# Q of two batches as fp32r products with late-loaded shared weights, and a transposed integer tail

## The chip, the core and the metric

The kernel runs on one core of one Trainium2 chip. The metric is the device time in microseconds (us) of one execution; lower is better. Five engines work side by side and wait for one another through semaphores: TensorE (PE; its weight loads are listed as PEld), VectorE (DVE), ScalarE (ACT), GpSimd (POOL) and SyncE (SP), which only issues transfers. Each engine runs its own instructions in their order.

## The reference, cut to what matters

Sixteen batches of 112 tokens of width 256 (`x`), each with a context of 375 rows (`ctx_1024`), pass four stages:

```
x = x + attention(layernorm(x), ctx, Wq, Wk, Wv, Wo) + bo     # 16 heads of 64
x = x + expert_ffn(layernorm(x)) + shared_ffn(layernorm(x))   # hidden 1024
x = x + softmax(layernorm(x) @ ctx.T / 16, masked) @ ctx      # one head of 256
x = x + int8_linear(layernorm(x))
```

The last line finds one scale for the whole tensor (the largest magnitude of the normalised x, over 127), divides and rounds to integers, multiplies by an int8 weight, and multiplies each output column by `x_scale * weight_scale` before the bias is added.

## The kernel before

**Attention.** One batch has two halves, c = 0 and 1, of eight heads each; half number u = 2b + c. While a half computes scores, softmax and the mix with V, TensorE also projects Q, K and V for the next half. These projections are cut in eight units of one PSUM bank each: unit 0 is Q (`Q_UNIT`, L1624 to L1631), units 1 to 4 are K, 5 to 7 are V (L1633 to L1649). Even units use bank 0, odd units bank 1. K and V are done as three fp32r products of high and low parts (`split_products`), so their weights and the context are kept as a high and a low part each. Q is one plain fp32 product: four pairs of heads times two row tiles, with the tokens `xn_t` of one batch (112 columns) moving. A Q or K unit is evicted by ScalarE (high part, L754 and L756) and then VectorE (low part, L1099 and L1103); both halves of the bank's release go through `proj_used`.

A half has two visits v = 0 and 1 of four heads each. In each, TensorE does the scores (L1662), the mix of the visit before (L1696), and then four times: transposes of one head's probabilities (`turn_probs`, L1677) and one unit. After visit 1 come the output projection (L1717), which waits for `heads_split`, that is for VectorE's `heads_rest` (L1129), and a turning of tokens (L1609). Head i's transposes wait for the copy of an earlier head out of the bank (L1671 to L1675): head 1 for VectorE's first copy (L1123).

VectorE's list in a visit is fixed by `batch` at L1147: maxima of two heads (L1112), in visit 0 of c = 1 the statistics of layernorm 2 and the context's low part (`ctx_rest`, L1018), maxima of the other two, copies of turned probabilities, reciprocals, the units' low parts, small steps of layernorm 2 (`norm2_steps`), `heads_rest`, and at the end the update of x (L1135). GpSimd multiplies the probabilities by the reciprocals (L664), two heads' worth after each pair of reciprocals, and in visit 1 of c = 1, from batch 2 on, it also issues the scatter of tokens (L672) between the first and the second of its four products.

The batches are unrolled for b = 0, 1 and 15; b = 2 to 14 is a loop of one batch.

**FFN.** The shared weights (`FFN_PIECE`, `FFN_PIECE + 1`) are loaded into `stage` and split in batch 0: `piece_hi` on ScalarE (L741) and `piece_lo` on VectorE (L1010), two halves for each piece. The tokens of the first FFN segment are split by `split_shared(0)` at L1218, in the last batch's c = 0.

**Tail.** The second attention runs one batch t a step; VectorE then does the statistics and extremes of layernorm 4 (`last_stats`). After it: moments, thirteen small steps (`norm_op`), a GpSimd all-reduce, scales, quotients (L980 on ScalarE, L1556 on VectorE), clipping and rounding (`quantise`, L1564 and L1569), transposes (L1993), integer products with tokens as the stationary side (L2006), the scale on VectorE (L1577) and the sum with `x_biased` on GpSimd (L726) or VectorE (L1586). `x_biased` is x plus bias, made on GpSimd (L705). Each of the four groups of four batches goes through this chain.

## Time and profile before

| | us |
|---|---|
| median of three runs | 957.97 (956.17 to 958.02) |
| profiled execution, its own time | 958.77 |
| its span, first to last instruction | 956.0 |
| TensorE busy | 903.7 (95%) |
| VectorE busy | 623.0 (65%) |
| ScalarE busy | 525.6 (55%) |
| GpSimd busy | 268.2 (28%) |

The profiled execution took 2.77 us more than its span, and 0.80 us more than the median. A profile lists, for each instruction, its start and length, and for idle time of an engine what ended it. The first attention fills the span from about 24 to 667 us, the FFN up to about 868, the second attention up to about 925, the tail the rest.

### The profile page before, as it was taken

What the parts mean: (1) busy time and instruction counts of PE and PEld (TensorE: products, weight loads), DVE (VectorE), ACT (ScalarE), POOL (GpSimd) and SP (SyncE); (2) the same over time, 40 slices, a digit from 0 to 9 for tenths busy, and PEclk for the clock granted to TensorE, in tenths of its full rate; (3) what the DMA queues carried; (4) which work ended last, traced back from release to release, by engine and by line L of the source; (5) the groups of instructions that cost most, each with busy time, mean ns of one, the idle gap of its engine ahead of it and who ended that gap; (6) DMA issues with size and microseconds to landing.
All of it is one profiled execution on the core that took longest, in us unless ns stands there. A gap on an engine that the chain in (4) does not pass through costs nothing.

```text
span 956.0 us, 19821 instructions
## 1 busy us (share of the span) xinstructions
PE 903.7 (95%) x6730; PEld 794.5 (83%) x6730; DVE 623.0 (65%) x1634; ACT 525.6 (55%) x1258; POOL 268.2 (28%) x337
## 2 busy tenths in 40 slices
PE   5889999999999999999999999998989999998864
PEld 4779888898888988889898898887878999996643
DVE  6766666767667676676766767665654666348777
ACT  4655565555655556555565555654742555446633
POOL 1323333333333333333433334333100000041214
PEclk9999999999999999999999999999999999999985
DMA  9230000000000000000000000000550142265502
GB/s 290 97 106 17 2 18 5 21 16 5 16 5 21 16 5 16 5 21 16 5 16 5 21 14 7 0 5 9 162 190 20 54 169 85 63 193 163 155 6 77
DMA packets 29459, 50.56 MB, mean 53 GB/s; under 512 B 2480, under 2 KB 24080, under 8 KB 27648
## 3 DMA queue, kind: packets, MB, share of 16 engines
q1 hardware_dynamic: 27888, 46.42, 15.6%
q0 software_dynamic: 1536, 3.67, 1.3%
q8 instruction: 21, 0.34, 0.2%
q14 instruction: 14, 0.11, 0.0%
HBM read 41.83 MB, written 8.26 MB: 52 GB/s over the span
## 4 chain that ended last, share of the span: by engine, by line
PE 88%; DVE 7%; ACT 2%; issue 2%; DMA 1%; POOL 0%; DVEq 0%
PE bank L1648 27%; PE bank L1677 10%; PE bank L1841 9%; PE bank L1696 9%; PE bank L1861 8%; PE bank L1662 8%; PE bank L1630 6%; PE bank L1717 5%; PE bank L1950 2%; PE bank L1968 1%; DVE norm_stats L1023 1%; PE bank L1811 1%; PE bank L1609 1%; PE bank L1957 1%; DMA x_all<-in_x 1%
## 5 line engine op out<-in xcount | busy, mean ns | idle before, releaser
L664 POOL TENSOR_TENSOR probs<-probs,row_rcp 112x375 f32<-112x375 f32 x256 | 202.4, 813 | 415.8 <-DVE row_rcp L1118 415.3
L784 ACT ACTIVATE probs<-bank,neg_max 112x375 f32<-112x375 f32 x256 | 144.4, 570 | 69.0 <-DVE neg_max L1112 68.9
L1677 PE MATMUL bank<-ident,probs 112*125 112x112 f32 x768 | 129.1, 277 | 2.3 <-DVE probs_t L1123 2.3
L1677 PEld LDWEIGHTS bank<-ident,probs 112*125 112x125 f32 x768 | 113.8, 187 | 18.2 <-issue 3.3
L1112 DVE TENSOR_REDUCE neg_max<-bank 112x1 f32<-112x375 f32 x256 | 123.3, 539 | 7.6 <-PE bank L1662 7.5
L1123 DVE COPY probs_t<-bank 125x336 f32<-125x336 f32 x128 | 64.7, 506 | 70.1 <-PE bank L1677 66.8
L756 ACT ACTIVATE k_parts<-bank 128x376 fp32r<-128x376 f32 x128 | 62.1, 485 | 69.3 <-PE bank L1648 69.3
L1648 PE MATMUL bank<-ctx_hi,wk_hi 128*128 128x376 f32 x256 | 97.2, 380 | 2.3 <-DVE k_parts L1103 1.5
L759 ACT ACTIVATE v<-bank 125x512 f32<-125x512 f32 x96 | 57.4, 598 | 57.2 <-PE bank L1648 57.1
L1696 PE MATMUL bank<-probs_t,v 125*64 125x112 f32 x1536 | 87.7, 263 | 0.6 <-ACT probs_t L772 0.6
L1696 PEld LDWEIGHTS bank<-probs_t,v 125*64 125x64 f32 x1536 | 74.0, 137 | 16.9 <-issue 16.7
L1103 DVE TENSOR_TENSOR k_parts<-bank,k_parts 128x376 fp32r<-128x376 f32 x128 | 69.9, 547 | 27.8 <-ACT k_parts L756 27.5
L1648 PE MATMUL bank<-ctx_lo,wk_hi 128*128 128x376 f32 x256 | 85.5, 334 | 0.0
L1648 PE MATMUL bank<-ctx_hi,wk_lo 128*128 128x376 f32 x256 | 85.3, 333 | 0.0
L1648 PE MATMUL bank<-wv_hi,ctx_hi 128*125 128x512 f32 x192 | 83.5, 435 | 0.0
L1662 PE MATMUL bank<-k_parts,q_parts 64*112 64x376 f32 x768 | 82.1, 345 | 0.0
L1648 PE MATMUL bank<-wv_hi,ctx_lo 128*125 128x512 f32 x192 | 75.8, 395 | 0.0
L1648 PE MATMUL bank<-wv_lo,ctx_hi 128*125 128x512 f32 x192 | 75.6, 394 | 0.0
L1662 PEld LDWEIGHTS bank<-k_parts,q_parts 64*112 64x112 f32 x768 | 61.2, 171 | 12.6 <-issue 7.9
L1412 DVE TENSOR_TENSOR hid_lo<-hid,hid_hi 128x448 fp32r<-128x448 f32 x72 | 45.0, 625 | 39.4 <-ACT hid_hi L915 34.2
L1630 PE MATMUL bank<-xn_t,wq_sb 128*128 (+1 forms) x512 | 65.9, 284 | 3.1 <-DVE x_all L1135 2.6
L1630 PEld LDWEIGHTS bank<-xn_t,wq_sb 128*128 128x128 f32 x512 | 62.9, 200 | 3.9 <-DVE x_all L1135 2.8
(208 smaller groups left out, 1877.0 us busy)
## 6 DMA issues: line engine op xcount, KB each, us to landing
stage<-in_ffn_up SPq DMA_DIRECT2D x6, 1024.0 KB, 5.4
stage<-in_ffn_down SPq DMA_DIRECT2D x6, 1024.0 KB, 7.5
ctx_raw<-in_ctx_t SPq DMA_DIRECT2D x16, 375.0 KB, 3.4
ring_late<-in_ctx_t SPq DMA_DIRECT2D x10, 375.0 KB, 6.8
ring_late<-in_ctx_n SPq DMA_DIRECT2D x10, 375.0 KB
routed<-xn SPq DMA_DIRECT2D x1, 2240.0 KB, 11.1
rows_in<-routed SPq DMA_DIRECT2D x5, 448.0 KB, 6.1
answers<-y_rows SPq DMA_DIRECT2D x10, 224.0 KB, 2.7
```

The costliest lines, as they stand in the source:

```text
L664: eng.tensor_tensor(probs[s][:, :], probs[s][:, :], row_rcp[:, s:s + 1].broadcast_to([S, C]), ALU.mult).then_inc(probs_ready, 1)
L784: eng.activation(probs[r][:, :], SCORE_BANKS[i][0:S, 0:C], ACT.Exp, bias=neg_max[:, r:r + 1], accum_out=row_sum[:, r:r + 1]).then_inc(exp_ ...
L1103: eng.tensor_tensor(k_parts[cf][:, 1, k - K_UNIT, :], bank[k % 2][:, 0:CP], k_parts[cf][:, 0, k - K_UNIT, :].bitcast(F32), ALU.subtract) \
L1112: eng.tensor_reduce(neg_max[:, r:r + 1], SCORE_BANKS[k][0:S, 0:C], AX.X, ALU.max, negate=True) \
L1123: eng.tensor_copy(probs_t[i][:, :, :], turn_bank(i, project)[0:CJ, 0:JT * S] .rearrange("p (j s) -> p j s", j=JT)).then_inc(probs_t_ready[ ...
L1630: m = eng.matmul(bank[0][:, p * S:(p + 1) * S], wq_sb[:, kt, col:col + P], xn_t[:, kt, bf, :], start=(kt == 0), stop=(kt == KT - 1))
L1648: m = eng.matmul(dest, wp, ap, start=(n == 0), stop=(n == 3 * KT - 1))
L1662: m = eng.matmul(SCORE_BANKS[2 * p + e][0:S, 0:CP], q_parts[c][heads[e], a, 2 * v + p, :], k_parts[c][heads[e], b, 2 * v + p, :], start=(i ...
L1677: t = eng.transpose(turn_bank(i, project)[0:CJ, j * S:(j + 1) * S], probs[QUAD * v + i][:, j * CJ:(j + 1) * CJ], ident[0:S, 0:S])
L1696: m = eng.matmul(HEADS_BANK[DH * e:DH * e + DH, (s // 2) * S:(s // 2 + 1) * S], v_sb[c][:, j, s * DH:(s + 1) * DH], probs_t[2 * p + e][:, ...
L1841: mm = eng.matmul(bank[n % 3][:, 0:GT], wp, ap, start=(i == 0), stop=(i == 3 * KT - 1))
L1861: mm = eng.matmul(down_banks(s)[k][:, 0:GT], wp, ap, start=(m == 0 and i == 0), stop=(m == MT - 1 and i == 2))
```

## The change

1. **Q of two batches.** From batch 2 on, Q is made for batches b and b + 1 together, as three fp32r products with 224 columns moving, in two units (`PAIR_UNIT` = -1 and `Q_UNIT` = 0) of two pairs of heads each. A pair of batches has four halves; the projections done in them are then of 9, 7, 7 and 9 units (in the order even c = 0, even c = 1, odd c = 0, odd c = 1), where before each had 8. In a half of 7, K stands in the first slot, and the last slot has none; in a half of 9 the last slot holds V units 6 and 7. Tokens are normalised and turned two batches ahead; ScalarE writes their high part (`pair_out`), VectorE their low part (`pair_rest`), which is put right after the first two maxima of visit 0 in c = 1. The loop body is two batches.
2. **Shared weights late.** The split Q and K weights live where the FFN's shared weights go. The split of Wq takes the place of the first piece's in batch 0; the second piece's in batch 0 goes away. The first piece is split at the end of batch 14, the second in visit 0 of the last half, where `split_shared(0)` now also stands.
3. **Tail.** The moments of layernorm 4 are taken inside the loop over t. The integer weights become the stationary side, four products of 448 columns for each group in place of eight of 256. ScalarE scales and adds the bias in one instruction, TensorE turns the result back by fp32 transposes, VectorE adds it to x. GpSimd keeps only the product of the two scales.

```diff
@@ units and order
+                    self.queries = 2 if r % 4 < 2 else 0
+                return {1: [[k] for k in range(8)],
+                        2: [[PAIR_UNIT], [Q_UNIT], [1], [2], [3], [4], [5], [6, 7]],
+                        0: [[1], [2], [3], [4], [5], [6], [7], []]}[self.queries]
@@ scalar, batch
-                        if first and v == 1:
-                            piece_hi(FFN_PIECE + c)
+                        if first and c == 0 and v == 1:
+                            for h in range(2):
+                                eng.activation(piece_half(wq_hi, h), piece_half(wq_sb, h), ACT.Copy) \
+                                   .then_inc(wq_rounded, 1)
...
+                        elif v == 1 and t is not None:
+                            pair_out(t, t % 2 if isinstance(t, int) else odd)
...
+                        if isinstance(b, int) and b == B - 2 and c == 1 and v == 1:
+                            piece_hi(FFN_PIECE)
+                        if last and c == 1 and v == 0:
+                            piece_hi(FFN_PIECE + 1)
@@ vector, batch
                         largest_scores(visit, v, 0)
+                        rest = rest_for(b, c)
+                        if v == 0 and rest is not None:
+                            pair_rest(rest, rest % 2 if isinstance(rest, int) else odd)
...
-                        if first and v == 1:
-                            piece_lo(FFN_PIECE + c)
+                        step_rest(3)
+                        if isinstance(b, int) and b == B - 2 and c == 1 and v == 1:
+                            piece_lo(FFN_PIECE)
...
-                        if last and c == 0 and v == 1:
-                            eng.wait_ge(proj_ready[0], unit_count(u + 1, 4))
+                        if last and c == 1 and v == 0:
+                            eng.wait_ge(proj_ready[1], units.all(1))
                             split_shared(0)
+                            piece_lo(FFN_PIECE + 1)
@@ tensor, unit
+                if k <= Q_UNIT and f.queries == 2:
+                    for i in range(2):
+                        col = (PAIRS * cf + 2 * (k - PAIR_UNIT) + i) * P
+                        for kt in range(KT):
+                            w = [t[:, kt, col:col + P] for t in (wq_hi, wq_lo)]
+                            a = [t[:, kt, :] for t in (xq_hi, xq_lo)]
+                            for wp, ap in split_products((w, a)):
+                                m = eng.matmul(bank[k % 2][:, 2 * i * S:2 * (i + 1) * S], wp, ap, start=(n == 0),
+                                               stop=(n == 3 * KT - 1))
@@ tail
-        VECTOR_RATIOS = (2, 2, 1, 1)
+        VECTOR_RATIOS = (2, 2, 2, GB)
...
+            def answers_out(i):
+                for part in (slice(0, GT),) if i < NG - 1 else (slice(0, 2 * S), slice(2 * S, GT)):
+                    for k in range(KT):
+                        eng.activation(out_t[i][:, k, part], bank[2 * (i % 2) + k][:, part], ACT.Identity,
+                                       scale=out_scale[:, k:k + 1], bias=qb_col[:, k:k + 1]).then_inc(out_t_ready, 1)
...
+            def add_answers(i):
+                for h in range(2):
+                    b = GB * i + 2 * h
+                    eng.wait_ge(out_turned, 2 * i + h + 1)
+                    eng.tensor_tensor(result[i][:, 2 * D * h:2 * D * h + 2 * D].rearrange("s (b d) -> s b d", b=2),
+                                      x_all[:, b:b + 2, :], bank[4 + h][0:S, :].rearrange("s (b d) -> s b d", b=2),
+                                      ALU.add).then_inc(result_ready, 1)
...
+                for n in range(KT):
+                    for k in range(KT):
+                        m = eng.matmul(bank[2 * (i % 2) + n][:, 0:GT], wi[:, k, n * P:(n + 1) * P],
+                                       xi_t[i % 2][:, k, :], start=(k == 0), stop=(k == KT - 1))
+            for i in range(NG):
+                turn_integers(i)
+                if i >= 1:
+                    products(i - 1)
+                if i >= 2:
+                    turn_answers(i - 2)
+            products(NG - 1)
+            turn_answers(NG - 2)
+            turn_answers(NG - 1)
```

## Rows read from the trace of the kernel before

**Rows 1.** The page: busy time and share of each engine, and the last chain.

```profile
PE 903.7 (95%) x6730; PEld 794.5 (83%) x6730; DVE 623.0 (65%) x1634; ACT 525.6 (55%) x1258; POOL 268.2 (28%) x337
...
PE 88%; DVE 7%; ACT 2%; issue 2%; DMA 1%; POOL 0%; DVEq 0%
```

**Rows 2.** Timeline, TensorE, one half c = 1: start us, length us, engine, line, operation.

```profile
407.97 1.27 PE L1662 MATMUL bank<-k_parts,q_parts 64*112 64x376 f32 x12
...
410.89 1.95 PE L1630 MATMUL bank<-xn_t,wq_sb 128*128 x16
412.67 0.49 PE L1677 MATMUL bank<-ident,probs 112*125 112x112 f32 x3
...
416.87 1.30 PE L1662 MATMUL bank<-k_parts,q_parts 64*112 64x376 f32 x12
```

**Rows 3.** The same timeline, neighbouring fp32r products, one after the other.

```profile
406.97 0.28 PE L1717 MATMUL bank<-wo_hi,heads_hi 128*112 128x256 f32 x1
407.09 0.28 PE L1717 MATMUL bank<-wo_lo,heads_hi 128*112 128x256 f32 x1
...
413.53 0.33 PE L1648 MATMUL bank<-ctx_hi,wk_hi 128*128 128x376 f32 x1
413.70 0.34 PE L1648 MATMUL bank<-ctx_lo,wk_hi 128*128 128x376 f32 x1
```

**Rows 4.** Timeline, VectorE, the same half.

```profile
410.19 0.93 DVE L1018 TENSOR_TENSOR ctx_lo<-ctx_raw,ctx_hi 128x752 fp32r<-128x752 f32 x1
...
411.95 0.50 DVE L1123 COPY probs_t<-bank 125x336 f32<-125x336 f32 x1
```

**Rows 5.** Timeline, batch 14's c = 1: TensorE, GpSimd and VectorE around the output projection.

```profile
607.54 1.27 PE L1662 MATMUL bank<-k_parts,q_parts 64*112 64x376 f32 x12
...
622.20 2.35 POOL L664 TENSOR_TENSOR probs<-probs,row_rcp 112x375 f32<-112x375 f32 x3
...
621.90 2.68 DVE L1043 TENSOR_TENSOR norm_term<-norm_bits 112x1 f32<-112x1 f32 x1
...
625.08 0.62 DVE L1129 TENSOR_TENSOR heads_lo<-bank,heads_hi 128x448 fp32r<-128x448 f32 x1
...
625.79 0.34 PE L1717 MATMUL bank<-wo_hi,heads_hi 128*112 128x256 f32 x1
```

**Rows 6.** Groups by line and form: count, busy us, mean ns, idle before them.

```profile
L1010 DVE TENSOR_TENSOR up_lo<-stage,up_hi 128x1024 fp32r<-128x1024 f32 x12 | 14.6, 1219 | 1.1 <-ACT up_hi L741 1.1
...
L741 ACT ACTIVATE up_hi<-stage 128x1024 fp32r<-128x1024 f32 x12 | 12.5, 1055 | 0.0
```

**Rows 7.** Timeline, VectorE and GpSimd, the last batch.

```profile
644.31 0.62 DVE L1142 CAST xs_hi<-xn_t 128x896 fp32r<-128x896 f32 x1
644.97 1.09 DVE L1144 TENSOR_TENSOR xs_lo<-xn_t,xs_hi 128x896 fp32r<-128x896 f32 x1
...
652.81 1.91 DVE L1112 TENSOR_REDUCE neg_max<-bank 112x1 f32<-112x375 f32 x4 [1.36 <-PE bank L1662]
...
651.05 3.12 POOL L664 TENSOR_TENSOR probs<-probs,row_rcp 112x375 f32<-112x375 f32 x4 [7.39 <-DVE row_rcp L1118]
```

**Rows 8.** Timeline, TensorE, the first Q unit of batch 1, after an idle stretch.

```profile
70.14 3.57 PE L1630 MATMUL bank<-xn_t,wq_sb 128*128 128x112 f32 x16 [2.57 <-DVE x_all L1135]
```

**Rows 9.** Timeline, VectorE and TensorE, the tail.

```profile
932.38 1.38 DVE L1556 TENSOR_SCALAR ratio<-x_all,norm_moments,ratio_scale 112x256 f32<-112x256 f32 x4
...
939.25 1.64 DVE L1569 TENSOR_SCALAR xi<-ratio 112x1024 bf16<-112x1024 f32 x1
...
951.81 1.20 DVE L1586 TENSOR_TENSOR ring_late<-ring_late,x_biased 112x512 f32<-112x512 f32 x1
...
946.24 3.62 PE L2006 MATMUL bank<-wi,xi_t 128*112 128x256 bf16 x16
```

**Rows 10.** Busy time by stretch: engines (count), granted clock, DMA share, GB/s.

```profile
70.00:74.00 4.00, 3.86 (x20) 3.86 (x21) 2.39 (x7) 2.03 (x7) 1.47 (x2) 0.58 0.00 0
...
945.00:950.00 5.00, 4.34 (x24) 3.93 (x24) 4.31 (x6) 0.92 (x1) 3.71 (x3) 0.50 0.38 118
```

More of the change, by code:

```diff
@@ new lines, in halves, with tokens_for, rest_for @@
+        def halves(pair, odd, last):
+            b = pair + odd
+            return [(c, 2 * b + c, not (last and c == 1), b + c, Units(pair, 2 * odd + c), Units(pair, 2 * odd + c + 1))
+                    for c in range(2)]
+        def tokens_for(b, c):
+            if isinstance(b, int) and b < 2:
+                return {(0, 0): 1, (0, 1): 2, (1, 0): 3}.get((b, c))
+            return b + 2 if c == 0 and not (isinstance(b, int) and b + 2 >= B) else None
+        def rest_for(b, c):
+            if c == 1:
+                return tokens_for(b, 0) if not (isinstance(b, int) and b == 0) else None
+            return 2 if isinstance(b, int) and b == 1 else None
@@ L785, in exponential, with batch @@
                                bias=neg_max[:, r:r + 1], accum_out=row_sum[:, r:r + 1]).then_inc(exp_ready, 1)
-            def batch(b, first=False, last=False):
-                for c, u, project, _ in halves(b, last):
+            def batch(pair, odd, first=False, last=False):
+                b = pair + odd
+                for c, u, project, _, units, later_units in halves(pair, odd, last):
+                    steps = later_units.steps()
                     for v in range(2):
@@ L1145, in split_shared, with batch @@
                    .then_inc(xs_ready, 1)
-            def batch(b, first=False, last=False):
+            def batch(pair, odd, first=False, last=False):
+                b = pair + odd
                 second_batch = isinstance(b, int) and b == 1
                 later = not first and not second_batch
-                for c, u, project, bf in halves(b, last):
+                for c, u, project, bf, units, later_units in halves(pair, odd, last):
+                    steps = later_units.steps()
                     for v in range(2):
@@ L1719, in project_out, with batch @@
                 m.then_inc(wo_ready, 1)
-            def batch(b, first=False, last=False):
+            def batch(pair, odd, first=False, last=False):
+                b = pair + odd
                 second_batch = isinstance(b, int) and b == 1
                 later = not first and not second_batch
-                for c, u, project, bf in halves(b, last):
+                units_ago = Units(pair, 2 * odd - 1) if odd else before(pair)
+                for c, u, project, bf, units, later_units in halves(pair, odd, last):
+                    steps = later_units.steps()
                     for v in range(2):
```

487 lines of the change are left out of this document (271 added, 216 removed).

## The prediction

> **What bounds the kernel now.** I read the page first, then TensorE's timeline of one steady half, then VectorE's and GpSimd's of the same stretch, and last the two ends. TensorE is busy 95% of the span and carries 88% of the last chain [rows 1]. So its instructions have a price, unless another engine is right behind it. That second question decides this change. In a steady half c = 1 the scores start at 407.97 and those of visit 1 at 416.87, 8.90 us later [rows 2]; the next half of that kind, 607.54 on, has its output projection at 625.79, 18.25 us after its start [rows 5]. Two neighbours come close to TensorE there. In visit 0, VectorE's first copy of turned probabilities starts at 411.95, behind the context's low part at 410.19 [rows 4], 3.98 us into the half; TensorE needs it done before the second head's transposes, which start at 412.67, 4.70 us in [rows 2]. In visit 1, VectorE's layernorm step at 621.90 takes 2.68 us where it is a single column; it ends at 624.58, as GpSimd's three products end (622.20 + 2.35 = 624.55) [rows 5]. `heads_lo` follows at 625.08 to 625.70, and the projection at 625.79. So the half c = 1 is already held by GpSimd through VectorE, 0.1 us behind TensorE's own work.
>
> **The products.** Q now: 16 instructions between 410.89 and 412.67, 1.78 us for a half, 112 ns each [rows 2]. Two batches have four halves: 7.12 us. After: 24 products with 224 columns for each of two halves, 48 in all. Their rate is not in the trace. From below: fp32r products start 117 ns apart (256 columns; 0.12 in the rows) and 170 ns apart (376 columns) [rows 3], about 0.44 ns a column, which gives 103 ns at 224 columns. From above: Q's own 112 ns, for weight loads of the same 128 x 128 shape. I take 112, the row of the same weights: 48 x 0.112 = 5.38 us a pair, 1.34 us a unit. The gain on TensorE alone is 1.74 us a pair, 12.2 us over the seven pairs (15.3 by 103 ns).
> The Trainium skill ("TensorE: Matmul & The Clock Gate", LDWEIGHTS) gives a weight load as its columns over 1.2 GHz, by which an estimate for 128 columns is 107 ns. The sum would then be 48 x 0.107 = 5.14 us a pair. The 112 ns of Q's rows agree with it, and no row shows it for 224 columns.
>
> **The four halves of a pair, step by step.** Before: ten halves lie between 407.97 [rows 2] and 607.54 [rows 5], 19.96 us each; c = 1 takes 20.0 and c = 0 19.9, 79.8 for a pair. K slot: 1.12 us of products and 0.25 of transposes; V slot: 1.40 and 0.25 (estimates from the 170 ns of rows 3, and 232 ns read in the same way for 512 columns).
> - *Even c = 1, 7 units.* K is first, and with cf = 0 it waits for the context's low part. `pair_rest` (224 columns, 0.33 us by the spacing of VectorE's 376-column ops) stands ahead of it: it ends 3.4 us in, where TensorE wants it at 2.85. The second transposes wait until 4.75 for the copy that now comes 0.33 later [rows 4]. With four K units visit 0 ends at 8.9, as before. So visit 1 starts as before, and so do exponentials and GpSimd's products, whose end frees VectorE at 17.0 us; `heads_lo` is done at 18.2. TensorE, with three V units, is ready for the projection at 16.9 and waits 1.4. The half stays at 20.0: nothing of its 1.78 is won.
> - *Odd c = 0, 7 units.* No scatter and no context. TensorE would need 18.0; `heads_hi` comes after the third head's copy on ScalarE and `heads_rest` after it, 16.3 us in, for a projection wanted at 15.95: 18.4.
> - *Even c = 0, 9 units.* 19.9 - 1.9 + 2.7 = 20.7. No wait added.
> - *Odd c = 1, 9 units.* 20.0 - 1.9 + 2.7, plus 0.56 until the copy at 4.75, less the 0.2 that Q waited: 21.1. Its own length hides GpSimd's.
> Sum 80.2: +0.4 for a pair, for six loop pairs +2.4. Bounds: with 103 ns it is -0.0 a pair; with the stalls of c = 1 at zero, -1.7; with `pair_rest` pushing twice as much, +1.2.
> GpSimd's hold on VectorE is what the row at 621.90 shows: an operation on a single column lasts until the last product of GpSimd ends [rows 5].
> The Trainium skill ("GPSIMD Engine Reference", Key points) says that GpSimd shares its SBUF interfaces with VectorE, with contention for VectorE instructions in a two-port mode or with two SBUF inputs. The step at L1043 has two. By that rule, the stall in the even c = 1 stays whatever TensorE saves there; the trace agrees in the 2.68 us.
>
> **The edges of the attention.** *Batches 0 and 1.* The first split stays where it was (now Wq). Dropping the second's is worth little: tokens of batch 2 are turned and copied on ScalarE before `wo_hi`, so x is updated some 0.25 us earlier than in the wait of 2.57 us before the Q unit at 70.14 [rows 8]. Batch 1's c = 1 has 9 units: +0.9 and the wait of 0.5: +1.4. Sum +1.2.
> *Batch 14.* Its c = 0 has 9 units: +0.8; its c = 1: 0.
> *First piece, between 14 and 15.* `piece_hi` is two halves of 1.055, after the last token copy, `piece_lo` two of 1.22 [rows 6], ahead of x's update and the next maxima. They end some 4.0 us into the half, the four maxima take 1.9, and the copy that head 1's transposes need is done at 6.7 where TensorE is there at 3.97: +2.75. The 7-unit half gives 1.5 back: +1.3. Nothing covers it, since VectorE's list is fixed. An idle stretch of that length once put Q to 3.57 us [rows 8], with a granted clock of 0.58, between the levels of 1.2 and 2.4 GHz [rows 10]; half of that loss, 0.8, I add.
> *Second piece, last half.* No projections here, so VectorE's list is the path. Before, it is free from 651.45 to the maxima at 652.81 [rows 7]. Added: `split_shared(0)` (0.62 + 1.09) [rows 7] and 2 x 1.22 [rows 6], 4.15 us, behind ScalarE's 2.1 and beside GpSimd's products of 3.12 [rows 7]. Without contention the maxima start at 655.8 (+3.0), with all of GpSimd's run in front +5.3. I take +4.0, between them; every later wait is on this chain. In the half before, `split_shared` had been free, so nothing comes back.
> Attention: 2.4 + 1.2 + 0.8 + 1.3 + 0.8 + 4.0 = +10.5.
>
> **The tail.** Moments in the loop remove 0.9 us at its end and two extremes (0.2 each) leave the thirteen steps: layernorm 4 is ready 1.4 earlier. The twelve moments of 0.16 in a loop that VectorE and TensorE tie cost half of their time back, 0.8. After the scales (932.38 before) the end goes by TensorE: at the 0.50 clock of this stretch [rows 10], with 226 ns for 256 columns (3.62 over 16) [rows 9], a group's four products take 4 x 0.395 = 1.6 us, its eight fp32 transposes 1.6 (twice the 0.1 each that the same form takes in the FFN), its bf16 ones 0.72. GpSimd is silent, so rounding takes 0.7 in place of 1.64 [rows 9]. Replayed in TensorE's order from 930.95, T0 at 933.75, T1 at 935.85, the first products at 936.6, and from 938.7 without a gap: the last turned answers are there at 950.7, the last sum (0.65) at 951.4, where before it ended at 953.01 [rows 9]. The transfer behind it (3.0 to the span's end) is the same. If the full clock comes back at about 943, as TensorE now works without a break, the end is 2.4 earlier. So the sum is -1.6 (951.4 for 953.0, layernorm's 1.4 in it) + 0.8 lost in the loop = -0.8 at the half clock, and -3.2 with the full one; I take the middle, -2.0.
>
> **Sum.** +10.5 - 2.0 = +8.5 on the profiled 958.77 (its span of 956.0 and 2.77 around it): 967.3. That execution lies 0.8 over the median of 957.97, so the median after is 966.5; I say 966.
>
> **Rivals.**
> 1. *The gain arrives (not slower).* The c = 1 half shortens after all, because GpSimd's products and the copy of head 0 move forward with TensorE. Then the pairs give -1.7 x 6 = -10.4 in place of +2.4: 966 - 12.8 = 953. For it: TensorE is the chain nearly everywhere [rows 1]. Against: both waits hang on VectorE's list, which starts with the half. It decides from the point at which the projection in even c = 1 starts under 17.6 us after the scores. Chance 0.18.
> 2. *Half of it arrives*, by 103 ns a product and a shorter hold: -0.9 a pair, 966 - 7.8 = 958. Chance 0.12.
> 3. *VectorE as the bound in visit 0.* The low parts of two Q units crowd into a list that is full for the first 8 us; each c = 1 loses another 1.0 and each idle stretch takes clock as at 70.14 [rows 8]: 14 more halves of 0.5 on average, +7: 973. Chance 0.15.
> 4. *The products are no cheaper than fp32*, that is 149 ns or more each, so that the change does not do what it says: +12.2, 978. Rows 3 speak against it. Chance 0.03.
>
> **How the numbers follow.** The forecast has the remaining 0.52, with 962 to 970 as its own range. To leave out no more than 2 in 10, the range takes rival 2 and most of rival 3 and ends above rival 1's centre: 954 to 973. About 0.2% (1.9 us) is what a measurement here can tell from no change, 956.1 to 959.9. Faster: rival 1 and a third of rival 2, 0.22. Same: most of the rest of rival 2, 0.09. Slower: 0.69.
>
> **What would show it.** In the profile after: `PAIR_UNIT` products 103 to 112 ns apart; the halves of a pair near 20.7, 20.0, 18.4 and 21.1 us; in even c = 1 a wait of TensorE for `heads_lo` over 1 us; a wait of 2 to 3 us at the start of batch 15 for a copy of probabilities; the maxima of the last visit 3 to 5 us after the scores; the quotients 0.6 us nearer the second attention's end. I am wrong if the even c = 1 half takes under 19 us, or if the pieces' VectorE work lies in idle time.

## The result and the profile after

The changed kernel takes 982.09 us (median, 980.41 to 982.63) beside 957.4 of the kernel before on the same chip: a ratio of 1.0265, 95% interval 1.0247 to 1.0283. The forecast was 966. The sign was right; the size was not. The profiled execution took 982.25 us with a span of 980.5, which is 24.5 over the span of before.

First the page of the changed kernel, the busy times and the last chain, to be read against [rows 1]:

```profile
PE 907.2 (93%) x6634; PEld 790.7 (81%) x6634; DVE 622.3 (63%) x1652; ACT 531.8 (54%) x1266; POOL 252.1 (26%) x325
...
PE 80%; DVE 13%; issue 4%; ACT 1%; DMA 0%; DVEq 0%; POOL 0%
```

The busy times are nearly the same. TensorE's part of the chain fell from 88 to 80%, and VectorE's rose from 7 to 13%. So waits came in. To find them I took the start of the scores of every half from TensorE's timeline, in both kernels. The table is worked out from these starts; "forecast" is the term of my sum, and for the four halves of a pair it has the forecast length in brackets.

| stretch | before | after | difference | forecast |
|---|---|---|---|---|
| start to the scores of batch 2 | 108.62 | 109.33 | +0.7 | +1.2 |
| even c = 0, nine units | 19.9 | 20.8 | +0.9 | +0.8 (20.7) |
| even c = 1, seven units | 20.0 | 20.2 | +0.2 | 0.0 (20.0) |
| odd c = 0, seven units | 19.9 | 18.3 | -1.6 | -1.5 (18.4) |
| odd c = 1, nine units | 20.0 | 23.2; 24.7 in batches 3 and 11 | +3.2; +4.7 | +1.1 (21.1) |
| batches 2 to 13, all | 479.0 | 498.0 | +18.9 | +2.4 |
| batch 14 | 39.9 | 40.6 | +0.7 | +0.8 |
| batch 15, c = 0 | 19.71 | 22.35 | +2.6 | +2.1 |
| last scores' half to the first FFN product | 17.77 | 24.14 | +6.4 | +4.0 |
| first FFN product to the end | 290.97 | 286.13 | -4.8 | -2.0 |

One row carries the miss: the odd c = 1. Three of the four halves of a pair came within 0.2 us.

The timeline of one odd c = 1, visit 1, in the changed kernel (start us, length us, engine, line, operation; in brackets the idle time ahead and what ended it): VectorE, GpSimd, TensorE.

```profile
431.80 0.54 DVE L1198 TENSOR_TENSOR k_parts<-bank,k_parts 128x376 fp32r<-128x376 f32 x1
432.25 0.15 DVE L1213 RECIPROCAL row_rcp<-row_sum 112x2 f32<-112x2 f32 x1
432.32 2.68 DVE L1131 TENSOR_TENSOR norm_term<-norm_bits 112x1 f32<-112x1 f32 x1
...
435.52 0.55 DVE L1198 TENSOR_TENSOR k_parts<-bank,k_parts 128x376 fp32r<-128x376 f32 x1
435.99 0.62 DVE L1224 TENSOR_TENSOR heads_lo<-bank,heads_hi 128x448 fp32r<-128x448 f32 x1
...
432.62 2.35 POOL L735 TENSOR_TENSOR probs<-probs,row_rcp 112x375 f32<-112x375 f32 x3
...
433.95 0.48 PE L1802 MATMUL bank<-ident,probs 112*125 112x112 f32 x3
436.13 0.50 PE L1773 MATMUL bank<-wv_hi,ctx_hi 128*125 128x512 f32 x1 [1.69 <-DVE k_parts L1198]
...
439.02 0.28 PE L1842 MATMUL bank<-wo_hi,heads_hi 128*112 128x256 f32 x1
```

The layernorm step of a single column takes 2.68 us, as in [rows 5]: it ends with GpSimd's three products (432.62 + 2.35 = 434.97). In the half of nine units, K units 3 and 4 fall into visit 1, so the low part of unit 4 (435.52) now stands in VectorE's list behind that step. It releases the PSUM bank that V unit 6 needs. TensorE finished its transposes and stood idle for 1.69 us. Before the change all low parts of K of c = 1 but one came in visit 0, and that one ahead of the step.

In batches 3 and 11 the same wait cost 1.5 us more. Granted clock (the column after POOL) right behind the wait, in batch 3:

```profile
187.00:191.00 4.00, 3.96 (x12) 3.13 (x13) 1.15 (x4) 0.60 (x1) 0.00 (x0) 0.66 0.00 0
```

There V's products start 0.43 us apart from 188.30 to 191.29, and 0.23 apart in the other odd halves. The four other odd halves have the same idle stretch and keep their speed behind it. In the trace of the third experiment, where this part of the code is the same, it is again batches 3 and 11 that take 24.7 us.

The even c = 1 waits as I had it, for `heads_lo`, here behind the same step (2.21 us long in this half, to 396.26, as GpSimd's products end at 396.24). Its visit 0 takes 9.13 us, before 8.90. The Q products start 0.11 us apart, which is the 112 ns that I took.

```profile
394.05 2.21 DVE L1131 TENSOR_TENSOR norm_term<-norm_bits 112x1 f32<-112x1 f32 x1
...
396.77 0.62 DVE L1224 TENSOR_TENSOR heads_lo<-bank,heads_hi 128x448 fp32r<-128x448 f32 x1
...
393.89 2.35 POOL L735 TENSOR_TENSOR probs<-probs,row_rcp 112x375 f32<-112x375 f32 x3
...
397.49 0.34 PE L1842 MATMUL bank<-wo_hi,heads_hi 128*112 128x256 f32 x1 [1.07 <-issue]
...
420.59 0.27 PE L1746 MATMUL bank<-xq_lo,up_hi 128*128 128x224 f32 x1
420.70 0.27 PE L1746 MATMUL bank<-xq_hi,up_lo 128*128 128x224 f32 x1
420.81 0.28 PE L1746 MATMUL bank<-xq_hi,up_hi 128*128 128x224 f32 x1
```

The last half, to be read against [rows 7]: VectorE, GpSimd, TensorE, and behind them the busy times of one stretch with its granted clock.

```profile
674.33 0.98 DVE L1237 CAST xs_hi<-xn_t 128x896 fp32r<-128x896 f32 x1
675.34 1.58 DVE L1239 TENSOR_TENSOR xs_lo<-xn_t,xs_hi 128x896 fp32r<-128x896 f32 x1
676.85 3.58 DVE L1098 TENSOR_TENSOR down_lo<-wq_sb,down_hi 128x1024 fp32r<-128x1024 f32 x2
680.35 1.90 DVE L1207 TENSOR_REDUCE neg_max<-bank 112x1 f32<-112x375 f32 x4
...
674.01 5.33 POOL L735 TENSOR_TENSOR probs<-probs,row_rcp 112x375 f32<-112x375 f32 x4 [6.11 <-DVE row_rcp L1213]
...
682.81 1.42 PE L1802 MATMUL bank<-ident,probs 112*125 112x112 f32 x6 [4.43 <-DVE probs_t L1218]
```

```profile
685.00:690.00 5.00, 4.96 (x36) 4.74 (x36) 0.42 (x1) 0.00 (x0) 2.17 (x3) 0.50 0.08 23
```

VectorE's four operations and GpSimd's four products (5.33 us, 3.12 in [rows 7]) lengthen each other. TensorE's wait grew from 0.36 to 4.43 us, my +4.0. What I had left out is behind it: TensorE works from 685.0 to 690.2 at the lower level of 1.2 GHz, 2.3 us more for the projection and the mix (5.16 us, before 2.86). The two make the +6.4.

The tail: two stretches of the end, granted clock 0.51 and then 1.00, where [rows 10] has 0.50.

```profile
965.00:970.00 5.00, 4.36 (x24) 2.44 (x25) 4.23 (x9) 3.39 (x6) 0.54 (x1) 0.51 0.01 3
970.00:975.00 5.00, 4.87 (x42) 3.74 (x40) 3.10 (x5) 4.59 (x9) 0.00 (x0) 1.00 0.41 128
```

### The profile page after: what moved, and what is told of

Same layout as the page of the kernel before. It is cut to its first block, busy times and chain, and to the rows that moved or that the text cites. A ratio compares the mean times of both kernels' runs of the same rounds, so it can differ in the third digit from the quotient of the medians.

```text
span 980.5 us, 19538 instructions
## 1 busy us (share of the span) xinstructions
PE 907.2 (93%) x6634; PEld 790.7 (81%) x6634; DVE 622.3 (63%) x1652; ACT 531.8 (54%) x1266; POOL 252.1 (26%) x325
## 4 chain that ended last, share of the span: by engine, by line
PE 80%; DVE 13%; issue 4%; ACT 1%; DMA 0%; DVEq 0%; POOL 0%
PE bank L1773 25%; PE bank L1984 9%; PE bank L2004 9%; PE bank L1802 8%; PE bank L1821 6%; PE bank L1787 6%; PE bank L1842 5%; PE bank L1746 3%; DVE norm_term L1131 2%; DVE neg_max L1207 2%; PE bank L2093 2%; PE bank L2111 1%; PE bank L1755 1%; DVE ctx_lo L1106 1%; DVE norm_stats L1111 1%
## 5 line engine op out<-in xcount | busy, mean ns | idle before, releaser
L735 POOL TENSOR_TENSOR probs<-probs,row_rcp 112x375 f32<-112x375 f32 x256 | 204.6, 821 | 440.8 <-DVE row_rcp L1213 438.9
L840 ACT ACTIVATE probs<-bank,neg_max 112x375 f32<-112x375 f32 x256 | 144.6, 570 | 79.8 <-DVE neg_max L1207 79.8
L1802 PE MATMUL bank<-ident,probs 112*125 112x112 f32 x768 | 131.4, 281 | 11.3 <-DVE probs_t L1218 11.0
L1773 PE MATMUL bank<-ctx_hi,down_hi 128*128 128x376 f32 x256 | 97.6, 381 | 5.0 <-DVE ctx_lo L1106 2.8
L1773 PE MATMUL bank<-ctx_hi,down_lo 128*128 128x376 f32 x256 | 86.0, 336 | 0.0
L1773 PE MATMUL bank<-ctx_lo,down_hi 128*128 128x376 f32 x256 | 85.5, 334 | 0.0
L1230 DVE TENSOR_TENSOR x_all<-x_all,bank 112x256 f32 (+1 forms) x32 | 13.5, 421 | 85.5 <-PE bank L1842 85.5
L985 ACT ACTIVATE hid<-bank,b_col 128x448 f32<-128x448 f32 x48 | 30.5, 636 | 62.2 <-PE bank L1984 61.8
```

What stands on the lines that cost most here:

```text
L735: eng.tensor_tensor(probs[s][:, :], probs[s][:, :], row_rcp[:, s:s + 1].broadcast_to([S, C]), ALU.mult).then_inc(probs_ready, 1)
L840: eng.activation(probs[r][:, :], SCORE_BANKS[i][0:S, 0:C], ACT.Exp, bias=neg_max[:, r:r + 1], accum_out=row_sum[:, r:r + 1]).then_inc(exp_ ...
L1773: m = eng.matmul(dest, wp, ap, start=(n == 0), stop=(n == 3 * KT - 1))
L1802: t = eng.transpose(turn_bank(i, project)[0:CJ, j * S:(j + 1) * S], probs[QUAD * v + i][:, j * CJ:(j + 1) * CJ], ident[0:S, 0:S])
```

## The experiments

Ratios are to the kernel before on the same chip, with a 95% interval. The experiments ran on other chips than the result; the median of the kernel before was 956.4 to 960.1 us on them, so a time is to be read by its ratio and not beside 957.4. Where a few us matter I go by the halves in the traces: the first two batches differ by up to 3 us from one execution to the next in the same code, but the halves of the loop repeat within 0.1 us.

**One: K4's low part ahead of the layernorm steps.**

```diff
                             if v == 0:
                                 norm_moments(norm2, 0)
+                            else:
+                                step_rest(1)
                             norm2_steps(b - 1, 7 * v, 7 * v + 4)
-                        step_rest(1)
+                        if not (c == 1 and v == 1 and not first and not last):
+                            step_rest(1)
```

> The changed kernel with one move in VectorE's list: in visit 1 of c = 1 the low part of the K unit that falls there (K4 in the odd batch) comes ahead of the layernorm steps. Theory A (the layernorm step, held until GpSimd's three products end, keeps K4's low part and with it a PSUM bank from TensorE): the odd half c = 1 falls from 23.2 to 21.1 to 21.4 us in all six loop batches, the clock dips of batches 3 and 11 (1.5 us each) go with the idle stretch, the even half stays at 20.2; total 982.1 - 6 x 2.0 - 3.0 = 967, within 965 to 970. Rival B (GpSimd's products hold every VectorE operation, not the layernorm step alone): K4's low part ends at the same time as now, the odd half stays above 22.7, total 979 or more. Rival C (TensorE's loss is its own, from nine units in eight places): no change, 982.

Measured: 969.15 us, ratio 1.0099 (1.0073 to 1.0124), span 965.4, 15.1 under that of the changed kernel. The odd c = 1 takes 21.2 us in all six pairs, batches 3 and 11 among them; the even one stays at 20.2. The six pairs take 483.2 us where they took 498.0: 14.8 of the 15.1. Its timeline:

```profile
423.77 0.55 DVE L1198 TENSOR_TENSOR k_parts<-bank,k_parts 128x376 fp32r<-128x376 f32 x1 [0.52 <-ACT k_parts L812]
424.24 1.60 DVE L1131 TENSOR_TENSOR norm_term<-norm_bits 112x1 f32<-112x1 f32 x1
...
423.46 2.35 POOL L735 TENSOR_TENSOR probs<-probs,row_rcp 112x375 f32<-112x375 f32 x3
...
427.92 0.28 PE L1845 MATMUL bank<-wo_hi,heads_hi 128*112 128x256 f32 x1
```

The low part now runs while GpSimd multiplies, in its usual 0.55 us; the step behind it ends when GpSimd ends, at 425.84. So it was not VectorE as such that was held, and rivals B and C fall. The clock's 1.5 us in two halves went with the idle stretch.

**Two: `heads_rest` ahead of them as well.**

```diff
                             else:
                                 step_rest(1)
+                                heads_rest(u - 1)
                             norm2_steps(b - 1, 7 * v, 7 * v + 4)
                         if not (c == 1 and v == 1 and not first and not last):
                             step_rest(1)
-                        if v == 1 and not first:
-                            heads_rest(u - 1)
+                            if v == 1 and not first:
+                                heads_rest(u - 1)
```

> The first experiment, and besides heads_rest ahead of the layernorm steps in the same visit. Theory A: heads_lo follows heads_hi at once, so the even half c = 1 loses its wait of 1.07 us for the projection; but the layernorm steps now end later, and the turning of the gathered tokens behind the projection waits for them by some 0.4 us: even half 20.2 to about 19.6, odd half no change, total 3 to 5 us under the first experiment, 962 to 964. Rival B: heads_lo takes until GpSimd's products end wherever it stands, the even half stays at 20.2 or grows, total as the first experiment or above.

Measured: 964.8 us, ratio 1.0053 (1.0034 to 1.0072), 4.4 us under the first experiment, where 3 to 5 were expected. The even c = 1 went from 20.2 to 19.45, the odd stayed at 21.2. (The spans, 964.8 and 965.4, differ by less than this, since the first two batches took 3.5 longer here.)

```profile
468.06 0.62 DVE L1224 TENSOR_TENSOR heads_lo<-bank,heads_hi 128x448 fp32r<-128x448 f32 x1 [1.71 <-ACT heads_hi L821]
468.60 0.15 DVE L1131 TENSOR_TENSOR norm_term<-norm_bits 112x1 f32<-112x1 f32 x1
...
466.13 2.35 POOL L735 TENSOR_TENSOR probs<-probs,row_rcp 112x375 f32<-112x375 f32 x3
...
468.78 0.34 PE L1846 MATMUL bank<-wo_hi,heads_hi 128*112 128x256 f32 x1
```

`heads_lo` starts 0.42 us before GpSimd ends and takes 0.62 all the same; the layernorm step after GpSimd takes 0.15, not 2.68. The held step has two inputs, both in SBUF; `heads_lo` and `k_parts` have one of their two in PSUM. It is not enough for a hold that everything lies in SBUF, as the trace of the changed kernel shows (VectorE and GpSimd, three places):

```profile
385.64 0.15 DVE L1123 TENSOR_SCALAR norm_var<-norm_moments 112x1 f32<-112x1 f32 x1
385.71 0.14 DVE L1125 TENSOR_SCALAR norm_half<-norm_moments 112x1 f32<-112x1 f32 x1
...
383.97 3.22 POOL L735 TENSOR_TENSOR probs<-probs,row_rcp 112x375 f32<-112x375 f32 x4 [9.80 <-DVE row_rcp L1213]
```

```profile
35.95 2.04 DVE L1111 BATCH_NORM_STATS2 norm_stats<-x_all 112x6 f32<-112x256 f32 x6
...
34.42 3.28 POOL L735 TENSOR_TENSOR probs<-probs,row_rcp 112x375 f32<-112x375 f32 x4 [4.76 <-DVE row_rcp L1213]
```

```profile
488.31 0.83 DVE L1172 TENSOR_SCALAR xn<-x_all,norm_moments,norm_bits 112x256 f32 x1
...
487.40 1.58 POOL L735 TENSOR_TENSOR probs<-probs,row_rcp 112x375 f32<-112x375 f32 x2 [0.25 <-DVE row_rcp L1213]
```

Layernorm steps with one input on a single column, and the statistics of 256 columns, run at their usual 0.15 and 0.41 us beside GpSimd's products. A `TENSOR_SCALAR` over 256 columns is held: 0.83 us, 0.41 alone. What separates these one-input operations no run here was made for. The Trainium skill ("GPSIMD Engine Reference", Key points) names VectorE instructions in a two-port mode or with two SBUF inputs as the ones that contend with GpSimd; these rows agree with it.

**Three: the pieces of the shared weights moved,** nothing else. The first piece's halves go to the two visits of batch 15's c = 0, `split_shared(0)` and the second piece to visit 1 of the last half (ScalarE's parts likewise).

```diff
-                        if isinstance(b, int) and b == B - 2 and c == 1 and v == 1:
-                            piece_lo(FFN_PIECE)
                         pair_rcp(visit, v, 2)
+                        if last and c == 0 and v == 1:
+                            piece_lo(FFN_PIECE, 1)
...
                         step_rest(1)
...
+                        if last and c == 0 and v == 0:
+                            piece_lo(FFN_PIECE, 0)
...
-                        if last and c == 1 and v == 0:
+                        if last and c == 1 and v == 1:
                             eng.wait_ge(proj_ready[1], units.all(1))
                             split_shared(0)
-                            piece_lo(FFN_PIECE + 1)
...
                             x_update(b - 1 if c == 0 else b, u - 1, SUM_BANK)
+                        if last and c == 1 and v == 1:
+                            piece_lo(FFN_PIECE + 1)
```

> The changed kernel with the splits of the shared weights alone moved: the first piece to batch 15's c = 0 (one half in each visit, where both engines stood idle), the second piece and the split of the first tokens from visit 0 to visit 1 of the last half. Theory A (the pieces cost because they lie ahead of maxima in VectorE's fixed list, and the idle stretch takes clock as well): batch 15's c = 0 falls from 22.35 to about 18.5 us, the last half (scores to the first FFN product) from 24.1 to about 18.5, total 982.1 - 3.8 - 5.6 = 972.7, within 971 to 975. Rival B (both engines have no idle time there; the pieces cost wherever they lie in the attention): under 4 us back, 978 or more.

Measured: 973.84 us, ratio 1.0143 (1.0096 to 1.019), span 971.7. Batch 15's c = 0 fell from 22.35 to 18.10 us, a little under the 18.5 expected. The last half fell from 24.1 to 20.6 only, against 18.5.

```profile
675.09 2.82 DVE L1239 CAST xs_hi<-xn_t 128x896 fp32r<-128x896 f32 x1
...
675.07 2.35 POOL L735 TENSOR_TENSOR probs<-probs,row_rcp 112x375 f32<-112x375 f32 x3
...
678.07 1.61 PE L1826 MATMUL bank<-probs_t,v 125*64 125x112 f32 x24
```

The cast, 0.62 us in [rows 7], took 2.82: it lies in SBUF on both sides, and I had put it beside GpSimd's products. It has a single input.

**Four: all moves together,** with the second piece spread otherwise, so that neither the cast nor a split of weights stands beside GpSimd's products.

```diff
-                        if last and c == 1 and v == 0:
-                            eng.wait_ge(proj_ready[1], units.all(1))
-                            split_shared(0)
-                            piece_lo(FFN_PIECE + 1)
...
                             x_update(b - 1 if c == 0 else b, u - 1, SUM_BANK)
+                        if last and c == 1 and v == 1:
+                            eng.wait_ge(proj_ready[1], units.all(1))
+                            split_shared(0)
...
             probs_out(4 * B - 1, 1, False)
+            piece_lo(FFN_PIECE + 1)
+            heads_rest(2 * B - 1)
             split_shared(1)
-            heads_rest(2 * B - 1)
```

> The second experiment's order in visit 1 of c = 1, the first piece in batch 15's c = 0 as in the third, and the second piece spread otherwise: the first tokens are split behind the x update of visit 1, and the second piece's low part comes after the last two copies of probabilities, ahead of the last heads_rest. Theory A (all that the changed kernel lost in the attention are places in VectorE's list): from the second experiment's span of 964.8 the half b15 c0 gives 4.2 (22.35 to 18.1) and the last half 5.2 (24.1 to 18.9): span 955.4, about as the kernel before less its tail's gain would be 953; ratio to the kernel before 0.994 to 0.998. Rival B (a piece's 4.4 us of VectorE and ScalarE work has no free place here, the wait comes back behind another operation): last half above 21, ratio 1.000 or more.

Measured: 955.03 us, ratio 0.9949 (0.9927 to 0.997), span 952.2. The last half takes 18.9 us, as expected, and the cast 0.62 again:

```profile
658.04 0.62 DVE L1239 CAST xs_hi<-xn_t 128x896 fp32r<-128x896 f32 x1
...
660.54 2.35 DVE L1100 TENSOR_TENSOR down_lo<-wq_sb,down_hi 128x1024 fp32r<-128x1024 f32 x2
```

Beside the kernel before, batch 15's c = 0 is 1.6 us shorter and the last half 1.1 longer, where the changed kernel had +2.6 and +6.4. So the pieces cost some 1 us where they stand beside neither GpSimd's products nor a copy that TensorE wants. The four moves of order took 28 us off the changed kernel's span.

**Five: the tail alone,** put on the kernel before. Its edit is the change's own: moments in the loop, `answers_out`, `turn_answers`, `add_answers`, and GpSimd's `out_scale`, in place of `rescale` and `add_bias`.

```diff
-            def rescale(i):
+            def add_answers(i):
...
-                                           xi_t[i % 2][:, KT * (2 * h + j) + k, :], wi[:, k, :],
+                        m = eng.matmul(bank[2 * (i % 2) + n][:, 0:GT], wi[:, k, n * P:(n + 1) * P],
+                                       xi_t[i % 2][:, k, :], start=(k == 0), stop=(k == KT - 1))
```

> The kernel before with the new tail alone (moments in the loop, transposed products, scale and bias on ScalarE, sum on VectorE), Q and the weights as they were. By the two traces the end of the FFN to the end of the span is 4.75 us shorter in the changed kernel. Theory A (the tail gains by itself): 957.4 - 4.8 = 952.6, within 951.5 to 954. Rival B (the gain needs the attention's timing or was the clock's chance in that execution, as the full clock came back at 970 in the trace): under 3 us gained, 955 or more. My forecast had -2.0, which would be 955.4.

Measured: 955.51 us, ratio 0.9954 (0.9929 to 0.9979), which is 4.4 us off with an interval from 2.0 to 6.8; its profiled span is 953.4, 2.6 under that of [rows 1]'s execution. From the scales (931.9 in both traces) to the end it took 21.4 us, before 24.1, in the changed kernel 20.5. From the first FFN product to the scales it took 266.7 against 266.9; my 0.6 for the moments can't be told there, since the nine traces with the new tail besides this one have 265.0 to 267.0. The full clock is there too, in the last five us of work:

```profile
945.00:950.00 5.00, 3.94 (x29) 2.81 (x27) 3.75 (x6) 3.31 (x7) 0.00 (x0) 1.00 0.77 240
```

So the tail is a gain by itself. The median is above the 954 of theory A, since the kernel before was slower on this chip, and the interval holds theory A's 4.8 as well as the "under 3" of rival B; this run doesn't decide between them. The ten traces with the new tail do better: from the first FFN product to the end they take 286.1 to 288.6 us (middle 288.0), where the one trace of the kernel before has 291.0. So the gain is 2.4 to 4.8 us, 3 in the middle, and the changed kernel's -4.8 is its upper end. Part of the -4.8 stands in the FFN and second attention (265.6 us from the first product to the scales in the changed kernel, 266.5 in the first experiment, whose code is the same there), so part of it is scatter.

**Six: one of three Q products left out** (low weights times high tokens; the answers lose that term), on the kernel of the second experiment.

```diff
-                            for wp, ap in split_products((w, a)):
+                            for wp, ap in split_products((w, a))[:2]:
                                 m = eng.matmul(bank[k % 2][:, 2 * i * S:2 * (i + 1) * S], wp, ap, start=(n == 0),
-                                               stop=(n == 3 * KT - 1))
+                                               stop=(n == 2 * KT - 1))
```

> The second experiment without the third product (low weights times high tokens) of the Q units of a pair: 8 of 24 products fewer in each nine-unit half, the answers less exact. 8 x 0.112 = 0.9 us of TensorE's work is gone from each. Theory A (with the layernorm step out of the way TensorE sets the nine-unit halves): even c = 0 from 20.84 to 19.95, odd c = 1 from 21.2 to 20.3, total 11 us under the second experiment (964.8), 954. Rival B (ScalarE's and VectorE's evictions of nine units set them): less than 0.4 us off each, 960 or more. Rival C (only c = 1 hangs on VectorE, through the copy that the second transposes wait for): c = 0 loses 0.9, c = 1 under 0.5.

Measured: 955.54 us, ratio 0.995 (0.9931 to 0.9969). The even c = 0 fell by 0.75 us (20.84 to 20.09), the odd c = 1 by 0.3 (21.2 to 20.9), for 0.9 us less of work in each. That is rival C. In the odd half the second transposes wait longer, 0.74 us here (first row) where the kernel with all moves has 0.28 (second fence):

```profile
331.44 0.58 PE L1806 MATMUL bank<-ident,probs 112*125 112x112 f32 x3 [0.74 <-DVE probs_t L1218]
```

```profile
331.38 0.58 PE L1810 MATMUL bank<-ident,probs 112*125 112x112 f32 x3 [0.28 <-DVE probs_t L1220]
```

TensorE sets the even c = 0. VectorE sets visit 0 of the odd c = 1, through its first copy of probabilities.

The whole fell by 10 us beside the second experiment, near theory A's 11, but not on its way: the six pairs give 6.2 and batch 14 0.7. Another 1.6 lies in batch 15's c = 0 (20.77 us for 22.34), where no Q is made. TensorE's wait of 2.44 us is the same in both traces and in that of the changed kernel; behind it the granted clock fell there (first line, changed kernel) and stayed here (second line).

```profile
656.00:660.00 4.00, 4.00 (x18) 4.00 (x17) 1.50 (x6) 1.87 (x4) 1.64 (x3) 0.58 0.00 0
```

```profile
631.00:635.00 4.00, 4.00 (x33) 3.52 (x31) 2.34 (x9) 2.14 (x5) 1.67 (x3) 1.00 0.00 0
```

**Seven: the kernel before with the tail and `heads_rest` first.** The control for the second experiment: the same move without the Q change.

```diff
                                 norm_moments(norm2, 0)
+                            else:
+                                heads_rest(u - 1)
                             norm2_steps(b - 1, 7 * v, 7 * v + 4)
...
-                        if v == 1 and not first:
+                        if v == 1 and not first and not (c == 1 and not last):
```

> The kernel before with the new tail (as in the fourth experiment) and heads_rest ahead of the layernorm steps in visit 1 of c = 1. Theory A (as I read the trace of before: that half was held 0.1 us behind TensorE's own work): 1.3 us under the tail alone, 954. Rival B (with the hold gone everything behind it moves up as well): 0.4 us or more a half, 13 halves, 5 us under it, 950. Rival C (the tokens' turning waits for the later layernorm steps): no gain or a loss, 955.5 or more.

Measured: 952.27 us, ratio 0.9918 (0.9894 to 0.9943). The half c = 1 went from 20.03 to 19.77, so 0.25 of it was held and not the 0.1 that I read in [rows 5]; 13 halves make 3.3 us, between A and B. Rival C falls.

**Eight: the first copy earlier.** The kernel with all moves; in visit 0 of c = 1 the context's low part goes behind the copy in the odd batch, and the copy goes ahead of the second two maxima in the even one.

```diff
+                        late_ctx = c == 1 and v == 0 and odd == 1 and later and not last
+                        early_copy = c == 1 and v == 0 and odd == 0 and later
-                        if project and c == 1 and v == 0:
+                        if project and c == 1 and v == 0 and not late_ctx:
                             ctx_rest(b + 1)
+                        if early_copy:
+                            probs_out(visit - 1, 0, project)
                         largest_scores(visit, v, 2)
-                        if turning:
+                        if turning and not early_copy:
                             probs_out(visit - 1, 0, project)
+                        if late_ctx:
+                            ctx_rest(b + 1)
```

> The kernel with all moves, and in visit 0 of c = 1 (batches 2 to 14) the first copy of probabilities earlier in VectorE's list: in the odd batch the context's low part goes behind the copy (its first K unit is the third there), in the even one the copy goes ahead of the second two maxima. Theory A (the second transposes wait for that copy, 0.28 us in the odd half and about 0.3 in the even one, and nothing else is late there): odd c = 1 from 21.2 to 20.9, even from 19.45 to 19.2, six pairs, 3.5 us in all: span 952.2 to about 949. Rival B (TensorE then waits for the next in the list, the second copy or the later exponentials): under 0.1 us a half, 952. Rival C (in the even half the exponentials of heads 2 and 3 come 0.5 later and so GpSimd's products and heads_hi): even half 19.6 or more, 952 to 954.

Measured: 947.51 us (946.71 to 948.39), ratio 0.9898 (0.9879 to 0.9916), span 946.6. The odd c = 1 went from 21.2 to 20.7 and the even one from 19.45 to 19.16. That is the lowest median and the lowest ratio of the study, and faster than both given kernels. Beside the seventh experiment, which has no Q change, it is not clear of noise: the intervals overlap (0.9894 to 0.9943 there), and the spans are 946.6 and 949.8. In the odd half the wait is gone, and the first transposes of that form take 0.48 again, not 0.58:

```profile
330.36 0.49 DVE L1220 COPY probs_t<-bank 125x336 f32<-125x336 f32 x1
330.77 0.93 DVE L1108 TENSOR_TENSOR ctx_lo<-ctx_raw,ctx_hi 128x752 fp32r<-128x752 f32 x1
...
331.31 0.48 PE L1816 MATMUL bank<-ident,probs 112*125 112x112 f32 x3
```

A wait of 0.28 in the trace gave back 0.5 us; which part of the restart makes the rest I did not separate. `ctx_rest` stays ahead of the reciprocals on purpose: it has two SBUF inputs, and behind them it would stand beside GpSimd's products.

**Nine: the same move in the kernel before,** on that of the seventh experiment, as a control.

```diff
+                        early_copy = c == 1 and v == 0 and later
+                        if early_copy:
+                            probs_out(visit - 1, 0, project)
                         largest_scores(visit, v, 2)
-                        if turning:
+                        if turning and not early_copy:
                             probs_out(visit - 1, 0, project)
```

> The kernel before with the new tail and heads_rest first, and in visit 0 of c = 1 the first copy of probabilities ahead of the second two maxima, as in the even half of the run before. It is the control for it: is that move worth anything without the pair units? Theory A (no: the fp32 Q unit of 1.78 us stands between the first and second transposes and covers the copy, which ended at 412.45 for transposes at 412.67): half c = 1 stays at 19.77, no change to the kernel with the tail and heads_rest first, ratio 0.990 to 0.994; the Q change is then worth its 5 to 6 us in the attention. Rival B (the move helps both kernels by 0.3 us or more a half): 4 us under it, ratio 0.988 or less, and the Q change gives next to nothing. Rival C (the later exponentials cost, since here no wait is won): slower, 0.994 or more.

Measured: 955.22 us, ratio 0.9952 (0.9925 to 0.998). The half c = 1 stays at 19.77, as theory A has it, so the move itself does nothing in the loop without the pair units. The whole came out slower than theory A's 0.990 to 0.994 and in the range of rival C. By the traces the last half starts 1.2 us later than in the seventh experiment, nearly all of it from the first two batches, which the edit does not touch, and its visit 0 went from 4.75 to 5.66, which is the edit's (it holds there too). The spans differ by 1.2 (951.0 and 949.8), the medians by 3; the intervals of the two ratios overlap.

## Why the forecast missed

**Right, by the halves.** The rate of the Q products (112 ns), the even c = 0 (20.8 for 20.7), the even c = 1 with a wait of 1.07 for `heads_lo` (I had 1.4) and nothing won (20.2 for 20.0; the 0.2 is in its visit 0, which I had at its old length), the odd c = 0 (18.3 for 18.4), and batch 14. In batch 15's c = 0 the wait less what seven units give back is +1.1 for my +1.3, and the clock 1.6 for my 0.8, by the sixth experiment's trace that lost no clock there. The hold on VectorE by GpSimd was read rightly from [rows 5] as to the layernorm step.

**Right by luck.** The start came to +0.7 for my +1.2, but the first two batches differ by up to 3 us in the same code. Inside it, batch 1's c = 1 took 2.1 more and not 1.4, and 0.6 of that went with K4's move (21.87 to 21.29 us): the step that failed, once more.

**The step that failed** is that of the odd c = 1: "Its own length hides GpSimd's." I asked of one operation behind the held step, `heads_lo`, whether TensorE would be late for it. I did not ask which others the nine-unit order puts there. K4's low part is one; it frees a bank in the middle of the visit, where no length of the half helps. Its price is +2.0 us in six halves and +1.5 twice for the clock, 15 us; the first experiment gave back 15.1. By the halves it is 14.8. Without it my own number for that half stands (21.2 for 21.1). Of the 16.0 us by which the span's +24.5 exceeds my +8.5, this step is 15.

**The second piece** was mis-sized by what comes after it: the wait grew by 4.1 for my +4.0, which was a middle taken between two bounds, but I added a clock loss only for the first piece, and here it took 2.3 us more. Experiments three and four show that the rest of the reasoning held: the 4 us came from the place and not from the work, and in the last half the place beside GpSimd's products mattered as much as that ahead of the maxima.

**The tail** was -4.8 in the two traces for my -2.0. I took the middle between an end at the half clock and one with the full clock back. It came back (1.00 from 970 on), and the fifth experiment's trace shows it as well, so the end with the full clock, -3.2, was the better one; the ten traces of the new tail have -3.0 in the middle.

**The rivals.** Rival 1 (the gain arrives, 953) hung on VectorE's list, as I wrote against it, and that was right: it decides there. With the list in another order part of it arrives: the pair takes 20.84 + 19.16 + 18.28 + 20.7 = 79.0 us, where the kernel before takes 79.8 and, with its own `heads_rest` moved, 79.35. So of the 1.74 us a pair that TensorE saves on Q, 0.8 arrives in the best order tried, and 0.4 against the better kernel before. Most of what doesn't arrive is in the even c = 1, which gains 0.6 of its 1.78 (19.16 for 19.77); what holds it there no run separates. Rival 3 had the right engine (VectorE) and the wrong visit. The range ended at 973 since it held no case in which a new order of units sets a bank's release behind a held operation.

**Open.** Behind the same idle stretch of 1.7 us the clock fell in two of six halves of one trace; it fell in the same two batches of the third experiment's trace, so they are not one execution's chance, but nothing here tells why it is those two. Behind the wait of 2.44 us in batch 15 it fell in three traces and not in a fourth. Nor is it settled how much of the Q change's gain is lasting once the kernel before has the better order.

## What to carry to other kernels

When an operation on an engine with a fixed list is found held, list everything that stands behind it in the new order, with the buffer that each one frees, and not only the operation that was behind it before. A saving on the busiest engine arrives only where the next engine's list leaves room: here four moves of order were worth 28 us, and the saved products, by the halves, 2.2 us over six pairs once both kernels have their better order. Put work with two inputs in SBUF, and long casts and scales from SBUF to SBUF, away from GpSimd's products, and operations that read PSUM beside them.

## What was new about the hardware

- The hold depends on what VectorE reads and from where, and size does not save an operation. A step on one column with two inputs in SBUF took 2.68 us (0.15 alone) beside GpSimd's products, a cast 2.82 (0.62 alone) and a `TENSOR_SCALAR` of 256 columns 0.83 (0.41 alone); operations with an input in PSUM took their usual 0.55 and 0.62, and one-input steps on a single column and the statistics their usual 0.15 and 0.41, all in SBUF as they were. It goes both ways: GpSimd's four products took 5.33 us in place of 3.12 where VectorE had long operations in SBUF. The Trainium skill ("SBUF — State Buffer", SBUF: two separate sides) calls the shared pair an exclusive lock held for a whole instruction. The rows agree that one side waits for the other; beyond what it says, the layernorm step was let in behind the last of three products in a row (434.97), not between two of them, though its own recorded start (432.32) lies 0.3 us ahead of the first.
- An idle stretch of TensorE of 1.7 us cost 1.5 us of clock in two of six like halves; one of 2.44 us was followed by a lower clock (0.58) in one trace and by 1.00 in another; one of 4.4 us was followed by five us at 0.50. A wait can have a second price, behind it.
- TensorE's clock came back to 1.00 within the tail, behind a stretch at 0.51 in which it was busy 4.36 of 5 us. The kernel before was busy 4.34 of 5 us at 0.50 [rows 10], but its work ended with that stretch.
